# Expert tiles ordered by the token group that opens them, with the last normalisation done behind the tiles

## What is computed

```python
shared = silu(x @ shared_gate.T) * (x @ shared_up.T) @ shared_down.T
probs = sigmoid(x @ router_w.T + routing_bias)            # 8 experts
scores, indices = top_k(probs, 2); scores /= sum(scores)
w = zeros((tokens, 8)); w[token, indices] += scores
g = silu(einsum('th,ehi->tei', xf, gate_w)); u = einsum('th,ehi->tei', xf, up_w)
combined = einsum('tei,eih,te->th', g * u, down_w, w)     # xf: x, flattened to tokens
out = layernorm(x + shared + combined)                     # no gain, no offset
```

## Time and profile before

| what | us |
|---|---|
| median of 3 runs | 1873.14 |
| range of the runs | 1871.34 to 1873.53 |
| the profiled execution's own time | 1876.15 |
| its span, first to last instruction | 1874.4 |
| TensorE (PE) busy in the span | 1713.3 (91%) |
| VectorE (DVE) busy | 1179.4 (63%) |
| ScalarE (ACT) busy | 802.0 (43%) |
| GpSimd (POOL) busy | 719.2 (38%) |

### The profile page before, as it was taken

How to read it: one execution, slowest core, us unless ns; L and a number is a source line. 1 busy time by engine, 2 the same in 40 slices (tenths; PEclk the granted TensorE clock), 3 DMA queues, 4 the chain that set the end, 5 groups by cost and what they waited for, 6 DMA issues and landing times.

```text
span 1874.4 us, 35484 instructions
## 1 busy us (share of the span) xinstructions
PE 1713.3 (91%) x9524; PEld 1435.8 (77%) x9525; DVE 1179.4 (63%) x2682; ACT 802.0 (43%) x1491; POOL 719.2 (38%) x625
## 2 busy tenths in 40 slices
PE   6999996999965999999999987999999999999980
PEld 4666655888864888888888875888888888888870
DVE  6777766888854667667677666555555555555546
ACT  5677766777721332322323334333333333333326
POOL 1011105888851243544435446233332333333333
PEclk9999997999996999999999998999999999999995
DMA  4444455777824222222122225333333333333329
GB/s 138 174 173 174 159 199 178 234 245 244 264 102 139 91 84 89 81 92 103 69 82 100 80 97 192 59 53 57 55 55 58 52 57 54 55 58 52 58 43 358
DMA packets 137705, 220.64 MB, mean 118 GB/s; under 512 B 40544, under 2 KB 110368, under 8 KB 129328
## 3 DMA queue, kind: packets, MB, share of 16 engines
q1 hardware_dynamic: 112064, 184.44, 30.1%
q0 software_dynamic: 25584, 35.54, 10.9%
HBM read 122.79 MB, written 97.12 MB: 117 GB/s over the span
## 4 chain that ended last, share of the span: by engine, by line
PE 44%; DMA 11%; issue 5%; POOL 5%; DVE 3%; ACT 2%; SPq 0%; POOLq 0%; ACTq 0%; another core or an unknown queue 0%; DVEq 0%
PE back_ps L2476 13%; DMA acc<-back_y,back_token 10%; PE back_ps L2496 7%; PE back_ps L2378 5%; PE back_ps L2364 4%; PE back_ps L2355 3%; PE back_ps L2274 3%; POOL back_turned_qk L1727 2%; POOL sorted L1715 2%; PE back_ps L2485 2%; PE back_ps L2309 2%; ACT back_out L1895 2%; PE back_ps L2317 2%; PE back_ps L2296 1%; PE back_ps L2262 1%
## 5 line engine op out<-in xcount | busy, mean ns | idle before, releaser
L2476 PE MATMUL back_ps<-back_w_gu,back_xe_T 128*128 x1620 | 413.0, 404 | 1.3 <-DVE back_xe_T L2212 1.3
L1758 POOL DMA_INDIRECT acc<-back_y,back_token x135 | 209.0, 1548 | 461.6 <-DVE back_y L2231 364.0
L2476 PEld LDWEIGHTS back_ps<-back_w_gu,back_xe_T 128*128 128x128 f32 x1620 | 297.5, 189 | 61.3 <-issue 2.3
L2496 PE MATMUL back_ps<-back_w_down,back_he_T 128*128 x1620 | 225.4, 288 | 1.5 <-DVE back_he_T L2224 1.5
L2496 PEld LDWEIGHTS back_ps<-back_w_down,back_he_T 128*128 128x128 f32 x1620 | 200.8, 189 | 1.8 <-issue 1.7
L1179 PE MATMUL front_ps<-front_xn_T,front_w_in_parts 128*128 128x512 f32 x768 | 186.6, 399 | 5.2 <-issue 3.3
L1715 POOL DMA_INDIRECT sorted<-back_x,back_slot x128 | 136.6, 1067 | 134.6 <-DVE back_slot L2044 100.3
L1010 DVE SCALAR_TENSOR_TENSOR front_conv<-front_ps,front_conv_wb,front_conv 128x508 f32<-128x508 f32 (+2 forms) x192 | 141.2, 742 | 63.4 <-ACT front_conv L842 58.9
L1179 PEld LDWEIGHTS front_ps<-front_xn_T,front_w_in_parts 128*128 128x128 f32 x768 | 143.3, 190 | 48.5 <-issue 18.5
L2220 DVE TENSOR_TENSOR back_h<-back_h,back_ps 128x512 f32<-128x512 f32 x135 | 92.7, 687 | 119.5 <-PE back_ps L2476 119.5
L1889 ACT ACTIVATE back_he_T<-back_ps 128x512 fp32r<-128x512 f32 x135 | 80.7, 598 | 200.2 <-PE back_ps L2485 200.2
(11 more groups left out here) (230 smaller groups left out, 3031.2 us busy)
## 6 DMA issues: line engine op xcount, KB each, us to landing
back_xe<-sorted SPq DMA_DIRECT2D x135, 136.0 KB, 2.5
gate_T<-front_gate_T SPq DMA_DIRECT2D x16, 1024.0 KB, 4.7
xc_T<-front_xc_T SPq DMA_DIRECT2D x16, 1024.0 KB, 5.7
front_xc_in<-xc_T SPq DMA_DIRECT2D x16, 1024.0 KB, 5.5
front_gate_in<-gate_T SPq DMA_DIRECT2D x16, 1024.0 KB, 6.5
front_x_rows<-in_x SPq DMA_DIRECT2D x16, 512.0 KB, 5.5
front_c_rep<-c_parts SPq DMA_DIRECT2D x128, 64.0 KB, 4.1
front_rows_in<-in_x SPq DMA_DIRECT2D x16, 512.0 KB, 7.3
```

The source lines that it names most:

```text
L1758: pool.indirect_dma_start(out=d["acc"][:, :], out_offset=bass.IndirectOffsetOnAxis(ap=token[:, r:r + 1], axis=0), in_=y[:, r % 2], in_offs ...
L2476: op = nc.tensor.matmul(dst[:, r % 2], xe_T[:, x_part, k], w_gu[:, bass.ds(e, 1), m, w_part, k], start=(n == 0), stop=(n == len(PASSES) - 1))
L2496: op = nc.tensor.matmul(ps_y[:, 0:D_MODEL], he_T[:, h_part, k], w_down[:, bass.ds(e, 1), w_part, k], start=(n == 0), stop=(n == len(DOWN_P ...
```

## The change

Tiles are numbered in the order in which the token groups open them: a tile of an expert is opened by the first group that has a row in it. `run` keeps its value after every group (17 x 8 numbers), the plan works on the 128 pairs of group and expert, and so has 11 operations, most of them 128 or 136 wide, and one more in `name_tiles` (`spare`). At most 8(g + 1) + 7 tiles hold the rows of groups 0 to g, so after that many adds the group's rows of `acc` are final.

A half group is 256 tokens; there are 32. From quad 5 (BEHIND) on, each quad carries one half group f = quad - 5:

```diff
+            if f is not None:                      # in in_tiles, between rows and up
+                half(f, r, last)
 # SP, r == 0, after the load of xe:
+                        if not is_at(f, 0):
+                            store_half(f - 1)      # waits half_out_ready; 256 KB
+                        sp.wait_ge(added, 16 * (4 * f + 15))
+                        sp.dma_start(half_in, d["acc_half"][f]).then_inc(half_loaded, 16)
+                        if last:
+                            sp.dma_start(end_in[0], d["acc_half"][f + 1]).then_inc(end_loaded[0], 16)
 # VectorE, r == 1: half_moments(f): waits half_loaded, 2 bn_stats, 2 bn_aggr; last quad also end_moments(0)
 # GpSimd, r == 1, after the add:
+            def half_root(f):
+                pool.wait_ge(half_mean_ready, HALF * (f + 1))
+                ...
+                nc.gpsimd.tensor_scalar(half_rstd, half_mean[:, :, 1], LN_EPS, None, ALU.add).then_inc(half_eps_ready, 1)
+                pool.wait_ge(half_eps_ready, f + 1)
+                nc.gpsimd.tensor_tensor(half_rstd, half_rstd, neg_half[:, 0:HALF], ALU.pow).then_inc(half_rstd_ready, 1)
 # VectorE, r == 2:
+                    dve.wait_ge(half_rstd_ready, f + 1)
+                    ...
+                    nc.vector.scalar_tensor_tensor(half_bias, half_mean[:, :, 0], -1.0, half_rstd, ALU.mult, ALU.mult
+                                                   ).then_inc(half_bias_ready, 1)
+                    if last:
+                        end_bias_of(0)
 # ScalarE, r == 3 (r == 2 in the last quad):
+                    act.wait_ge(half_bias_ready, f + 1)
+                    if not is_at(f, 0):
+                        act.wait_ge(half_stored, 16 * f)
+                    for s in range(HALF):
+                        nc.scalar.activation(half_out[:, s], half_in[:, s], ACT.Identity, scale=half_rstd[:, s:s + 1],
+                                             bias=half_bias[:, s:s + 1]).then_inc(half_out_ready, 1)
```

The smaller edits:

```diff
-                nc.vector.tensor_copy(token[:, r:r + 1], xe[:, r % 2, TOKEN_COL:TOKEN_COL + 1].bitcast(U32)
-                                      ).then_inc(row_ready, 1)
+                nc.vector.tensor_tensor(token[:, r:r + 1], xe[:, r % 2, TOKEN_COL:TOKEN_COL + 1], spare[:, bass.ds(i, 1)],
+                                        ALU.max).then_inc(row_ready, 1)
-                nc.vector.tensor_tensor(run, run, ps_small[:, GS * EXPERTS:(GS + 1) * EXPERTS],
-                                        ALU.add).then_inc(places, 1)
+                nc.vector.tensor_tensor(run[:, bass.ds(g + 1, 1)], run[:, bass.ds(g, 1)],
+                                        ps_small[:, GS * EXPERTS:(GS + 1) * EXPERTS].unsqueeze(1), ALU.add
+                                        ).then_inc(places, 1)
-        d["acc_rows"] = t["acc"][0:TOKENS].rearrange("(g p s) c -> g p s c", p=P, s=GS)
+        d["acc_rows"] = t["acc"][0:TOKENS].rearrange("(g h p s) c -> g p h s c", h=2, p=P, s=GS // 2)
+        d["acc_half"] = t["acc"][0:TOKENS].rearrange("(f p s) c -> f p s c", p=P, s=GS // 2)
-    nc = bacc.Bacc("TRN2", target_bir_lowering=False, num_devices=1)
+    nc = bacc.Bacc("TRN2", target_bir_lowering=False, num_devices=1, dynamic_dma_scratch_size=8192)
```

More of the change, by code:

```diff
@@ L1400, in decoder_back @@
         slot_f = at("slot_f", small + 2.3125, [P, 2, GS])
[L1401 to L1405, removed]
+        run = at("run", -1.75, [P, GROUPS + 1, EXPERTS])
+        count_i = at("count_i", -7.75, [P, GROUPS + 1, EXPERTS], I32)
+        tiles = at("tiles", -7.125, [P, GROUPS + 1, EXPERTS])
+        opened = at("opened", -6.5, [P, GROUPS, EXPERTS])
+        before_tile = at("before_tile", -6, [P, GROUPS, EXPERTS])
+        ends = at("ends", -5.5, [P, 3, GROUPS * EXPERTS])
+        columns = at("columns", 194.59375, [P, 2 * GS + 3])
+        spare = at("spare", -1.1875, [P, SLOT_TILES])
         neg_half = at("neg_half", 194.65625, [P, 2 * GS])
@@ L1563, in early, with in_quads, no_half, in_tiles @@
             return isinstance(g, int) and g < 2
+        def in_quads(eng, body):
+            body(0, False)
+            with eng.Fori(1, BEHIND) as quad:
+                body(quad, False)
+            body(BEHIND, False, 0)
+            with eng.Fori(BEHIND + 1, QUADS - 1) as quad:
+                body(quad, False, quad - BEHIND)
+            body(QUADS - 1, True, QUADS - 1 - BEHIND)
         def no_tile(i, r):
             pass
-        def in_tiles(eng, turn_x, up, turn_h, down, rows=no_tile):
+        def no_half(f, r, last):
+            pass
+        def in_tiles(eng, turn_x, up, turn_h, down, rows=no_tile, half=no_half, end_tile=2):
             rows(0, 0)
@@ L2068, in plan_tiles @@
                 dve.wait_ge(places, PLACES * GROUPS)
-                then(nc.vector.tensor_tensor(count_i, run, plan[:, PLAN_LESS], ALU.subtract))
+                last = EXPERTS - 1
+                less = plan[:, PLAN_LESS].unsqueeze(1)
+                at_ends = ends[:, 0].rearrange("p (g e) -> p g e", g=GROUPS)
+                end_steps = ends[:, 2].rearrange("p (g e) -> p g e", g=GROUPS)
+                rows_end = run[:, GROUPS:]
+                first_rows = before_tile.rearrange("p g e -> p (g e)")
@@ L2070, in plan_tiles @@
+                then(nc.vector.tensor_tensor(count_i, run, less.to_broadcast([P, GROUPS + 1, EXPERTS]), ALU.subtract))
                 then(nc.vector.tensor_scalar(count_i, count_i, 7, None, ALU.arith_shift_right))
                 then(nc.vector.tensor_copy(tiles, count_i))
-                then(nc.vector.tensor_tensor_scan(ends[:, 0], plan[:, PLAN_ONES], tiles, 0.0, ALU.mult, ALU.add))
-                then(nc.vector.tensor_scalar(ends[:, 1], tiles, -float(P), float(REGION), ALU.mult, ALU.add))
@@ L2074, in plan_tiles @@
-                then(nc.vector.tensor_tensor(ends[:, 2, 0:EXPERTS - 1], run[:, 1:], run[:, 0:EXPERTS - 1], ALU.subtract))
-                then(nc.vector.memset(ends[:, 2, EXPERTS - 1:], -1e6))
+                then(nc.vector.tensor_tensor(opened, tiles[:, 1:], tiles[:, 0:GROUPS], ALU.subtract))
+                then(nc.vector.tensor_tensor_scan(ends[:, 0], plan[:, PLAN_ONES], opened.rearrange("p g e -> p (g e)"), 0.0,
+                                                  ALU.mult, ALU.add))
+                then(nc.vector.tensor_tensor(before_tile, tiles[:, 1:], at_ends, ALU.subtract))
@@ L2076, in plan_tiles @@
+                then(nc.vector.tensor_tensor(end_steps[:, :, last:], rows_end[:, :, 0:1].to_broadcast([P, GROUPS, 1]),
+                                             rows_end[:, :, last:].to_broadcast([P, GROUPS, 1]), ALU.subtract))
                 assert n == PLANNED
@@ L2253, in _ @@
+            in_tiles(dve, turn_x, up, turn_h, down, rows, half)
+            for n in (1, 2):
+                end_moments(n)
+            for n in (1, 2):
+                end_bias_of(n)
         @block.tensor
```

209 lines of the change are left out of this document (137 added, 72 removed).

## The result

The changed kernel takes 1879.87 us (median of 6 runs, 1878.90 to 1881.93), the kernel before 1873.80 in the same runs: ratio 1.0033, 95% interval 1.0021 to 1.0046. Forecast were 1862.2 us, a range of 1844 to 1875, and a chance of 0.12 for slower. The profiled execution took 1879.57 us with a span of 1877.8, against 1876.15 and 1874.4.

The account below looks back on a forecast made before the run. TensorE was taken to bound the loop and an 8 MB read and store the end; -33.3 + 1.4 + 21 + 0 = -10.9 us took the median from 1873.14 to 1862.2, range 1844 to 1875.

Parts of the forecast that it names:

- The end: After the last add lands: load, moments, root, bias, two ACT operations and store take 16.9 us against 50.2, so -33.3.
- the last quad's +1.4: Last four tiles: VectorE's moments of two half groups and a `y` delayed behind the bias add 1.4 us.
- The main term: Tile loop, third tile of a quad: VectorE's `half_bias` waits for GpSimd's root, stalling 0.75 us, 28 times: +21.
- the moments: VectorE, second tile of a quad: 0.95 to 1.25 us of half-group statistics fit its idle time and slack, costing 0.
- The adds become the bound: Rival: GpSimd's root behind a late add costs the loop more than the end gives, from 1.14 us a quad; chance 0.13.
- Hidden: Rival: all the loop's new work is hidden, stall under 0.45 us a quad, 1844 at 0.1; chance 0.22.
- `xe` is nowhere late: Rival: half-group stores and loads delay `xe` loads, idling TensorE; 1876 at 0.5 us a quad more; chance 0.10, shared.
- The change does what it says: Rival denying this: tiles open later than the fixed wait on adds allows; given no chance of its own.
- The plan: Before the tiles: eleven wider operations delay weight passes 2.4 us, but scatters get ahead; 0, bounds -2.3 and +2.4.
- the row of 6.13: A scatter before the tiles taking 6.13 us during VectorE's weight passes, taken as evidence that those passes hold scatters.
- Order of the tiles: Tile loop: the new tile numbering costs 0; add landings shift by at most 0.2 us either way, inside the margin.
- Scratch: Half the DMA descriptor scratch: scatters keep 0.96 us and adds 1.55, so 0, bound +2.

Follow-up runs that it names:

- `owner_read_early`: The changed kernel, but TensorE reads the next tile's expert number before waiting for `h`; 1892.27 us, ratio 1.0101 to the kernel before.
- `order_only`: All of the change except the half groups and the split tile loop, with the old end; 1879.29 us, ratio 1.0032 to the kernel before.

## Why the prediction was wrong, point by point

**The end: right, a little small.** Forecast -33.3 and +1.4, measured -36.6. From the bias on I summed 0.2 + 1.2 + 5.1 = 6.5, and it took 3.9. The difference is the store: 5.1 was the last of sixteen at the end of 8 MB of traffic, and alone it took 2.6 (1875.2 to 1877.8). Of the last quad's +1.4, 0.36 shows, in the loop's stretch: the last interval of `h` is 5.22 in place of 4.86. Last `h` to last add is 7.61, and was 7.71.

**The loop: the mechanism was right, its size was not; this is the term that failed.** The main term, "1.15 late, of which 0.5 is slack: 0.65 of stall", times 28 with 0.1 for the lag, gave +21; it measured +34.5, or 1.24 a quad. `h` was placed nearly to the dot (1510.2 forecast, 1510.13 measured), and the transposes are 0.48 late, less than I said. What I missed is the step after: "TensorE waits for the first with its transposes, and the next `up` behind them" took it for granted that `up` keeps its 0.46 behind them. Once TensorE has waited, it is 0.96. That makes 0.98 of stall by the timeline and 0.94 by experiment (20.57 - 19.63), so 26 of the 34.5 us. The bytes are the second part: 0.21 a quad, 6 us, where I had 0.1 for a landing 0.7 longer; the landing is up to 1.7 longer. The remaining 0.09 a quad (19.63 - 19.54), 2.5 us, is the rest of the half groups' instructions: the moments, which I had at 0. 0.94 + 0.21 + 0.09 = 1.24. Taken away in the other order the wait is worth 0.77 (20.78 - 20.01) and the bytes 0.38: the two costs overlap in part.

**The rivals.** "The adds become the bound" said slower from 1.14 us a quad on, and named the place: GpSimd's root behind a late add, `half_bias` behind the root. The place is shown: the chain of waits runs over the adds, and `owner_read_early` makes them later still and loses. But adds alone do not carry it: without the bytes the same early wait costs 0.94 with the adds in time. It should have had more than 0.13, since my own stall of 0.75 lay only 0.39 from its point of decision, and one unpriced row was enough to cross it. "Hidden" fell. `xe` is nowhere late. The change does what it says.

**The plan, and what lies ahead of it: wrong, beyond its bound.** Forecast 0 with a bound of +2.4; the first `h` is 3.35 later in `order_only` and 5.5 in the changed kernel. The sum had no term for the steps: VectorE's last `place` is 2.9 and 3.4 late before the plan begins. The plan's own steps were right: it is 1.9 longer (3.25, and was 1.32), and the scatters get ahead. But before, the first tile waited for them and for its load of `xe` behind them (VectorE's first `w_row` stood idle for 4.88 until that landed); that wait is gone, and in its place the first tile waits for VectorE's weight passes, four of which take 4.3 us more beside GpSimd's. I had read the row of 6.13 as scatters held by VectorE, and had not asked what GpSimd would do next when they were not. What `order_only` and the changed kernel differ by, 2.2 us, goes with TensorE's granted clock: it is 1.00 and 0.72 between 1138 and 1144 us, 0.83 and 0.66 between 1124 and 1134, and six matmuls of the last group take 1.66 us in the one and 2.49 in the other. The same is seen in the other kernels: VectorE's weight passes start at 1143.8 to 1145.7 where that stretch is at 1.00, and at 1146.2 to 1148.1 where it isn't. Why the clock falls there in some executions isn't shown. The Trainium skill, page "SBUF — State Buffer", section "Who interferes with whom", has this rule: a VectorE instruction with two inputs in SBUF contends with a GpSimd instruction that reads SBUF. These rows agree (9.02 against 4.68, and the pair of 2.19 and 4.66).

**Order of the tiles: right. Scratch: at its bound.** `order_only` has the loop of before to 0.04 us. The scratch is +0.12% (0.03 to 0.22), some 2 us, where I had 0 with a bound of +2. The base stores had 0 too, and no run separates them from the rest of what makes the steps longer.

**The signs.** The period of one tile in four was to be 5.6 and is 6.00 (mean; median 5.88); "I am wrong if periods grow in other tiles too": one did, the second, 5.04 in place of 4.88. VectorE waited for an add before `w_row` once in 1300 to 1800, for 0.4 us, so that sign did not show. Weight passes "2 us later" were 7.3 later, from 1138.87 to 1146.18.

## What to carry to other kernels

An engine that waits in the middle of its stream loses the wait and its own start behind it: look for what follows the waiting instruction at a distance that held only while the queue was full. Put a new wait behind the work that others stand waiting for: here one moved line was worth 21 us. And when something is freed earlier (here GpSimd), name what it will do next and whom that meets; and before speeding up the engine that seems to be the bound, see whether the chain one step behind it can follow.

## What the runs showed of the hardware

- After TensorE had waited for `h`, register-addressed matmuls behind the transposes came 0.96 us after them, with 0.55 idle put down to "issue"; with the register read ahead of the wait, 0.43.
- An accumulating DMA of a tile lands in 3.8 us, but in 5.2 to 5.5 when 512 KB of plain loads and stores go out in the same tile, with the DMA engines busy for only 0.42 of the stretch; with the load and the store two tiles apart, 5.0 at most; with 1/128 of the bytes, 4.1.
- Two-input VectorE passes beside two-input GpSimd passes slow each other: 2.34 to 4.5 for two of the one, 4.87 to 6.51 for two of the other; even an operation on one column took 2.19 in place of 0.22.
- TensorE's granted clock differed between executions of kernels with the same steps: 1.00 in 1138 to 1144 us of `order_only`, 0.72 in the changed kernel, where six matmuls took 2.49 us in place of 1.66.
